# Three pairs of buffers for the spreads of the last layer, stored two steps at a time

## The reference

```python
def gcn_conv(x, W, b, row, col, n_nodes):
    xw = x @ W
    deg = jax.ops.segment_sum(ones, col, num_segments=n_nodes)
    dinv = jnp.where(deg > 0, jax.lax.rsqrt(deg), 0.0)
    norm = dinv[row] * dinv[col]
    msgs = norm[:, None] * xw[row]
    return jax.ops.segment_sum(msgs, col, num_segments=n_nodes) + b

h = jax.nn.relu(gcn_conv(x, W1, b1, row, col, n))
h = jax.nn.relu(gcn_conv(h, W2, b2, row, col, n))
x = _layernorm(x + h, axis=-1)
```

## Time and profile before

| | |
|---|---|
| Median of 3 runs | 19856.78 us |
| The profiled execution | 19880.46 us (span 19878.6 us) |
| PE, DVE, ACT, POOL busy | 46%, 84%, 31%, 66% |
| DMA | 1095.99 MB, mean 55 GB/s |
| The first spread (k = 0) | evictions from 8103.7 to 8778.3 us |
| The spreads of the last layer | evictions from 16119.5 to 16691.0 and from 18045.5 to 18613.0 us |

### The profile page before, as it was taken

The page is one execution under the profiler, slowest core; times in us unless marked ns, Lnnn a source line. Parts: engine busy times, 40 slices in busy tenths (PEclk is TensorE's granted clock), DMA queues, the critical chain, the costliest instruction groups (busy, mean ns, idle before and its releaser), DMA issues.

```text
span 19878.6 us, 288457 instructions
## 1 busy us (share of the span) xinstructions
PE 9075.4 (46%) x63545; PEld 6845.3 (34%) x63546; DVE 16662.2 (84%) x22374; ACT 6250.4 (31%) x13799; POOL 13030.6 (66%) x13651
## 2 busy tenths in 40 slices
PE   0114110110113777532347777887888864336432
PEld 0114010100113666432235555555555543225322
DVE  9989999999998888755659999999999976665666
ACT  0000233333332555220005555555555553004200
POOL 0048777777777777777757777777777613770476
PEclk9655555555557999555558998888888865555555
DMA  1023444444522222552331111111111165345534
GB/s 18 0 54 24 29 32 33 33 33 30 32 20 50 47 47 47 171 162 69 84 52 13 13 13 13 13 13 13 13 13 13 12 156 188 79 74 190 163 79 68
DMA packets 1751558, 1095.99 MB, mean 55 GB/s; under 512 B 1217323, under 2 KB 1658124, under 8 KB 1750028
## 3 DMA queue, kind: packets, MB, share of 16 engines
q0 software_dynamic: 454272, 412.11, 18.9%
q1 hardware_dynamic: 1089532, 417.46, 8.5%
q10 hardware_dynamic: 207632, 265.14, 4.2%
HBM read 700.94 MB, written 391.12 MB: 55 GB/s over the span
## 4 chain that ended last, share of the span: by engine, by line
POOL 33%; DVE 25%; issue 16%; DMA 13%; DVEq 7%; PE 5%; ACT 1%; POOLq 0%; SPq 0%; ACTq 0%
POOL gat L784 17%; POOL pay L750 12%; DVE red L2516 12%; DMA srcs<-spread,nbx 9%; DVE srcs L2509 5%; DVEq L2515 4%; POOL srcs L806 4%; DMA spread<-srcs 3%; PE banks L1272 3%; DVE arena L1733 2%; DVE srcs L2505 2%; ACT srcs L1016 1%; DVEq L1803 1%; DVEq L2499 1%; DVE g_s L2500 1%
## 5 line engine op out<-in xcount | busy, mean ns | idle before, releaser
L784 POOL DMA_INDIRECT gat<-tab,nbr x3328 | 3511.2, 1055 | 2150.4 <-DMA nbr<-nbr_src 1136.4
L806 POOL DMA_INDIRECT srcs<-spread,nbx x2808 | 2654.7, 945 | 2312.0 <-DMA nbx<-from_src 1375.6
L784 POOL DMA_INDIRECT gat<-tab,pay x3328 | 3172.1, 953 | 1083.7 <-issue 821.4
L1416 PE MATMUL banks<-w2rows,dsts 128*128 128x384 f32 x6656 | 3021.2, 591 | 928.9 <-DVE srcs L2509 739.1
L750 POOL DMA_INDIRECT pay<-records,nbr x2560 | 2523.7, 986 | 798.2 <-issue 779.6
L2516 DVE TENSOR_REDUCE red<-srcs 128x160 f32<-128x2560 f32 x832 | 2346.2, 2820 | 76.1
L1272 PE MATMUL banks<-srcs,hot 128*128 128x96 bf16 (+1 forms) x11232 | 1148.1, 278 | 2742.7 <-DMA srcs<-spread,nbx 2651.4
L1201 PE MATMUL banks<-ident,arena 128*128 128x128 f32 x2240 | 433.2, 380 | 4224.2 <-DVE arena L1761 2807.0
L902 ACT COPY banks<-arena 128x1024 f32<-128x1024 f32 (+1 forms) x1508 | 1323.6, 879 | 3300.8 <-DVE arena L1761 1274.8
L2200 DVE TENSOR_TENSOR arena<-arena,banks 128x96 f32 (+2 forms) x2816 | 723.1, 257 | 1449.0 <-PE banks L1272 1155.5
L1272 PEld LDWEIGHTS banks<-srcs,hot 128*128 128x128 bf16 x11232 | 875.2, 134 | 3015.7 <-issue 1594.9
(11 more groups left out here) (392 smaller groups left out, 20625.4 us busy)
## 6 DMA issues: line engine op xcount, KB each, us to landing
spread<-srcs SPq DMA_DIRECT2D x936, 192.0 KB
dsts<-key_rows SPq DMA_DIRECT2D x234, 512.0 KB
spread<-srcs ACTq DMA_DIRECT2D x468, 204.0 KB
staged<-gat SPq DMA_DIRECT2D x416, 148.0 KB, 1.8
gat<-staged ACTq DMA_DIRECT2D x416, 148.0 KB
dsts<-key_rows ACTq DMA_DIRECT2D x117, 512.0 KB
gat<-tab,nbr POOLq DMA_INDIRECT x3328
gat<-tab,pay POOLq DMA_INDIRECT x3328
```

The source lines that it names most:

```text
L784: pool.indirect_dma_start(out=gatv(s, GC[pas])[:, t, :], out_offset=None, in_=TAB[pas], in_offset=bass.IndirectOffsetOnAxis(ap=row, axis=0 ...
L806: pool.indirect_dma_start(out=chunk_rows(s, c)[:, q, :], out_offset=None, in_=rows, in_offset=bass.IndirectOffsetOnAxis(ap=nbx[:, r, s * X ...
L1416: last = t_.matmul(bank[1 + 2 * (p % 2) + h][:, 0:384], hid_rows[:, s % 2, 2 * p + h, :], w2rows[:, :], start=True, stop=True)
```

## The change

For k = 1 and 2 the evictions go to three pairs of buffers in `acc`, in words 9,600 to 11,903. Each pair holds two steps. ScalarE waits once per pair, before its even step, for the landing of the pair's last store; SyncE issues one store of 384 KB after the odd step, 3,072 contiguous bytes per partition. The rows of both `spread` tensors are numbered differently for this: the two steps of a pair lie side by side for each partition, so in the spread of k = 0, whose buffers and stores stay single, each store writes runs of 1,632 bytes that lie 3,264 bytes apart. The chunk numbers follow, by the same instructions with other constants. GpSimd waits for three semaphores instead of four before the collects of the last layer. The key load of SyncE stays ahead of the store of each fourth step.

```diff
+PAIRS = 3
+PAIR_USES = XSTEPS // 2 // PAIRS
@@ buffers
+        def pair_rows(j, c):
+            size = 2 * XGPS * CHUNK_EDGES * 3 * c
+            return acc[:, 9600 + j * size // 2:9600 + (j + 1) * size // 2].bitcast(BF16).rearrange("p (a g c) -> p a g c", a=2, g=XGPS)
@@ SyncE, spread_moves
-                rows_v = rows.rearrange("(n p g) c -> p n g c", p=P, g=XGPS)
+                rows_v = rows.rearrange("(n p a g) c -> p n (a g c)", p=P, a=2, g=XGPS)
...
-                    sp.wait_ge(spread_read, n + (k * XSTEPS + 3))
-                    sp.dma_start(rows_v[:, bass.ds(n, 1), :, :],
-                                 chunk_rows(s % SLOTS, c).rearrange("p (a g) c -> p a g c", a=1)).then_inc(spread_out[s % SLOTS], 16)
+                    if s % 2:
+                        j = s // 2 % PAIRS
+                        sp.wait_ge(spread_read, n + (k * XSTEPS + 3))
+                        sp.dma_start(rows_v[:, bass.ds(i * (KEYS // 2) + s // 2, 1), :],
+                                     pair_rows(j, c).rearrange("p a g c -> p (a g c)").rearrange("p (n c) -> p n c", n=1)).then_inc(pair_out[j], 16)
@@ GpSimd, chunk_gather
-                for s in range(SLOTS):
-                    pool.wait_ge(spread_out[s], 16 * XITERS * (k + 1))
+                if k:
+                    for j in range(PAIRS):
+                        pool.wait_ge(pair_out[j], 16 * PAIR_USES * k)
+                else:
+                    for s in range(SLOTS):
+                        pool.wait_ge(spread_out[s], 16 * XITERS)
@@ ScalarE, spread_rows
-                    if k or not first or s >= SLOTS:
-                        act.wait_ge(spread_out[slot], i * (16 * KEYS // SLOTS) + 16 * (s // SLOTS + k * XITERS))
                     if k:
-                        s_.copy(chunk_rows(slot, c), banks[:, 2 * (s % 2):2 * (s % 2) + 2, 0:CHUNK_EDGES * c3]).then_inc(spread_read, 1)
+                        j, used = s // 2 % PAIRS, s // 2 // PAIRS + (k - 1) * PAIR_USES
+                        if s % 2 == 0 and (used or not first):
+                            act.wait_ge(pair_out[j], i * (16 * KEYS // 2 // PAIRS) + 16 * used)
+                        s_.copy(pair_rows(j, c)[:, s % 2, :, :], banks[:, 2 * (s % 2):2 * (s % 2) + 2, 0:CHUNK_EDGES * c3]).then_inc(spread_read, 1)
                         return
+                    if not first or s >= SLOTS:
+                        act.wait_ge(spread_out[slot], i * (16 * KEYS // SLOTS) + 16 * (s // SLOTS))
...
-                    act.dma_start(rows_v[:, bass.ds(n, 1), :, :],
+                    act.dma_start(rows_v[:, bass.ds(i * (KEYS // 2) + s // 2, 1), s % 2, :, :],
@@ VectorE, edge_list
-                v.tensor_scalar(low, got, P - 1, 1, ALU.bitwise_and, ALU.logical_shift_left)
-                v.tensor_scalar(high, got, CHUNK_MASK - (XGPS * P - 1), None, ALU.bitwise_and)
-                v.tensor_scalar(numbers[:, :], got, 7, XGPS - 1, ALU.logical_shift_right, ALU.bitwise_and)
+                v.tensor_scalar(low, got, P - 1, 2, ALU.bitwise_and, ALU.logical_shift_left)
+                v.tensor_scalar(high, got, CHUNK_MASK - (2 * XGPS * P - 1), None, ALU.bitwise_and)
+                v.tensor_scalar(numbers[:, :], got, 7, 2 * XGPS - 1, ALU.logical_shift_right, ALU.bitwise_and)
```

More of the change, by code:

```diff
@@ L67 @@
 assert KEY_ITERS * KEYS == XSTEPS and KEYS % SLOTS == 0
+PAIRS = 3
+PAIR_USES = XSTEPS // 2 // PAIRS
+assert KEYS % (2 * PAIRS) == 0 and PAIR_USES * PAIRS * 2 == XSTEPS
 XG = XSTEPS * XGPS
@@ L406, in resnorm_gnn_kernel @@
         spread_out = [sem(f"spread_out{s}") for s in range(SLOTS)]
+        pair_out = [sem(f"pair_out{j}") for j in range(PAIRS)]
         nbx_in = [sem(f"nbx_in{r}") for r in range(RING)]
@@ L687, in _ @@
                 sp.wait_ge(staged_out[s], 16 * ITERS)
-                sp.wait_ge(spread_out[s], 16 * 3 * XITERS)
+                sp.wait_ge(spread_out[s], 16 * XITERS)
+            for j in range(PAIRS):
+                sp.wait_ge(pair_out[j], 16 * 2 * PAIR_USES)
         N_LOADS = 18
@@ L1002, in spread_rows @@
                 c3 = 3 * c
-                rows_v = rows.rearrange("(n p g) c -> p n g c", p=P, g=XGPS)
+                rows_v = rows.rearrange("(n p a g) c -> p n a g c", p=P, a=2, g=XGPS)
                 keys_v = keys.rearrange("(m b) c -> m (b c)", b=SLOTS)
```

## The result

The changed kernel takes 19959.24 us, the median of 5 runs (19948.77 to 19966.16). The kernel before, beside it, takes 19862.25 us (19844.69 to 19869.48). The ratio is 1.0050, 95% interval 1.0035 to 1.0064: slower by about 97 us. The forecast was 19804, range 19768 to 19850. Both sign and range are missed.

What follows compares the result with a forecast made beforehand. It took the late spreads to be bound by the store ring, 4.88 us per four steps, with PE's floor beneath: 4.55 + 0.10 = 4.65 us. Saving 54 us, less 1 at spread ends, gave 19804 us, range 19768 to 19850.

Steps and rivals of the forecast that it cites:

- The ring: Late spreads, buffer store and eviction: both pair stores land within 4.86 and 5.31 us, so ScalarE's store waits go.
- The rival of the unfreed ring: Late spreads: the doubled store behind the key load takes over 5.31 us, say 5.9; only 7 us saved, 19851; chance 0.12.
- The floor of 4.55 us: Late spreads: PE's matmuls and serial sequencer work per four-step cycle, 0.33 us below the present 4.88.
- The register load: PE's window-word load behind the loop's branch: excess falls from 0.18 to 0.10 us a cycle, bounds 0 and 0.25.
- four in ten long: Assumed share of long register loads behind PE's loop branch, giving the excess of 0.10 us a cycle.
- The rival "loads stay as they are": PE's register loads in late spreads keep their 0.18 us excess; cycle 4.73, kernel 19823; chance 0.20.
- The smaller terms: Outside the late spreads' cycle: +1 us at their ends; 0 for first spread, chunk numbers and GpSimd's start waits.
- The end of the first late spread: GpSimd's first gather stands behind 192 KB more, 0.6 us at each of two spreads: +1 us.
- The first spread: The kernel's first spread, buffers and sizes kept, 1632-byte runs now a step apart in DRAM: taken as 0.
- The rival that it gets dearer: First spread's scattered stores land 0.8 us later in each of 117 cycles: 94 us against 53 gained, 19898; chance 0.10.

Runs made afterwards that it cites:

- e2: The changed kernel with the stores of the last spread alone cut to a quarter, 768 of 3,072 bytes per partition; 19893.8 us.
- e3: The changed kernel with the row numbers of before: still one 384 KB store per pair, but in runs of 1,536 bytes; 20003.0 us.
- e8: The changed kernel with the key loads of the last spread alone cut to a sixteenth of their bytes, stores whole; 19956.8 us.
- e4: The kernel before with six single buffers instead of four in the late spreads, one 192 KB store a step; 19840.8 us.
- e9: The changed kernel with SyncE's pair store in the late spreads' loop also waiting for PE's next step, 0.6 us later; 19836.7 us.
- e10: The changed kernel with SyncE's pair store in the loop waiting for PE's step n + 2, the end of the next group; 19871.0 us.
- e5: The changed kernel with one register load of two words per turn of PE's spread loop instead of two of one word, all spreads; 19952.0 us.
- e6: The kernel before with one register load of two words per turn of PE's spread loop, in all three spreads; 19901.8 us.
- e7: The kernel before with six single buffers in the late spreads and one register load of two words per turn, in all three spreads; 19893.9 us.
- e12: The changed kernel with the pair store also waiting for PE's next step, timed on another chip; 19837.9 us, median of 10, ratio 0.9975.

## Why the prediction was wrong

**The ring: right.** The wait for stores is gone from the late spreads, as the geometry said. The store behind the key load landed in 3.9 us (estimate 4.05, bounds 3.6 to 5.15; the lower one has no working, 3.95 - 0.5 would be 3.45). The rival of the unfreed ring is out. The key load was not issued straight behind the first store but 0.6 us after it.

**The floor of 4.55 us: right**, and it carries further than it was used. It was one cycle near the spread's start; the trace has its two loads at 0.30 and 0.32 us, so it was a quiet one, which the text doesn't say. Take 4.55 and add what the two loads have above 0.31 + 0.30:

| kernel, spread | loads, us | 4.55 + excess | cycle measured |
|---|---|---|---|
| before, first late | 0.48 / 0.30 | 4.72 | 4.90, 77 us of store waits |
| changed, first late | 0.61 / 0.75 | 5.30 | 5.27 |
| e2, quarter stores | 0.44 / 0.37 | 4.75 | 4.73 |
| e3, short runs | 0.74 / 0.74 | 5.42 | 5.38 |
| e8, thin keys | 0.74 / 0.60 | 5.28 | 5.24 |
| e4, six single | 0.43 / 0.30 | 4.67 | 4.67 |
| e9, half a step later | 0.31 / 0.31 | 4.56 | 4.66, 57 us of store waits |
| e10, two later | 0.32 / 0.42 | 4.68 | 4.80, 58 us of store waits |

Where no eviction waits for a store, the sum is right within 0.04 us. Where some do, it is 0.10 to 0.18 short. It does not carry to one load of two words: 4.55 - 0.61 + 1.03 = 4.97 for e5 and 4.72 for e6 and e7, where 5.19, 5.04 and 4.98 were measured.

**The register load: the step that failed.** The text took 0.10 us of excess a cycle for PE's register loads, bounds 0 and 0.25. Measured is 0.75. With it the forecast's own sum would be 4.55 + 0.75 = 5.30, that is 0.42 x 233.5 = 98 us slower. Three things were wrong in it. First, the upper bound was no bound: it held one load to be long, and as long as one single row, 0.56 us. But the earlier trace rows had a maximum of 733 ns for this instruction, so that bound alone should have been 2 x 0.43 = 0.86 us; the range would have reached 4.55 + 0.86 = 5.41, some 125 us slower. Second, the other load was kept at 0.30 because it had been short before. It was short where the key load was landing, and e8 and e9 show that key loads leave it nearly alone; with pairs a store came to stand there. The text even put that store's issue at 0.02 of the cycle, just ahead of that load, and looked only at the branch's load. Third, the load and the stores were treated as independent, with a share of "four in ten long". They are not: the store is issued when the evictions of the last group are done, and the load when PE's next group has been issued. In the changed kernel this holds their distance at 0.75 to 1.25 us in every turn, where the store's packets have just begun. A long load moves the next group, and the evictions and the store move with it.

That their place to each other is what costs is shown by e9 and e12, which move the store alone. Why a sequencer's load is slower when it starts behind a store's issue is not shown here, and stays open; e10 shows that reads of SBUF going on beside it don't suffice. Nor was it tried to move the load instead of the store.

**The rival "loads stay as they are"** had the Trainium skill's rule behind it: "SBUF — State Buffer", the section on two separate sides, by which engine and DMA ports cannot contend. By that rule e9 would have changed nothing. For this load no such separation is seen: 0.30 us before the first store, 0.80 after it, 0.31 again once the stores are moved. Whether a sequencer's load goes by an engine port at all no run shows, so it may be that the rule doesn't cover it. The reason that the text gave against the rival was right; it only didn't follow it far enough.

**The smaller terms** held. The end of the first late spread to the next one's start: 1354.5 us before, 1355.3 after (forecast: +1 for both spreads). The first spread: 0 taken, 0 within 0.2 us measured. The rival that it gets dearer, the only one placed on the slower side, is out, and so the chance of 0.07 for slower rested on the wrong mechanism.

## What to carry to other kernels

When a wait is to be removed, read what stands on the next floor at its worst row, not at its mean, and place each of its instructions on a clock of one cycle against every transfer of the new schedule. Two periodic things driven by the same event can keep their distance for the whole stage: 232 of 233 loads were over 0.5 us in the changed kernel, 4 of 233 in e9. A share between is then no safe middle, though it can happen (68 of 233 before). Where they collide, it is enough to move one: here one more wait on an idle queue, 0.6 us long, took 614.8 + 614.6 us of spreads to 546.6 + 542.3, 140 us less.

## What the runs showed of the hardware

- A register load from SBUF by PE's sequencer takes 0.30 us for one word and 0.55 for two when quiet. Behind the issue of a 384 KB store from SBUF it takes 0.80 when it starts at 0.8 us, 0.59 at 1.1, 0.31 or 0.47 at 1.5 and 0.30 from 1.7 on (table at e10); two words took 1.03. Beside a 512 KB load into SBUF alone, at a DMA share over 1, it took 0.30. The Trainium skill, "Runtime: NRT & Kernel Launch", in its part on instruction fetch, has about 200 ns a register, as a round trip. The second word fits that (0.24), the first does not, and the growth beside stores is not in it.
- Runs of 3,072 bytes against 1,536 in the same store of 384 KB: 5.27 against 5.38 us a cycle, 13 us in 614.
- The granted clock was 0.50 (1.2 GHz) from 16200 to 16300 in before, after and e9 alike, so it explains nothing of the difference.
